# A cross-attention kernel with a second, token-driven attention: token weighing, gathers and low parts moved among heads and engines

## The reference

```python
query = hidden_states @ Wq                       # (2, 1024, 640), 8 heads of 80
keyt, valt = enc @ Wk, enc @ Wv                  # enc: 2044 rows of the context
hs = _mha(query, keyt, valt)                     # the large attention
ca_q1 = jnp.einsum('btc,th->bch', ca, Wq_ca)     # ca: the last 4 rows of the context
indices = np.linspace(0, 383, 1024).astype(np.int64)
ca_q1 = ca_q1[:, indices, :]                     # 384 distinct rows, repeated to 1024
ca_hs1 = _mha(ca_q1, residual, residual)         # residual = hidden_states
ca_q2 = ca_hs1 @ Wq
ca_hs2 = _mha(ca_q2, ca @ Wk_ca, ca @ Wv_ca)     # only 4 keys
out = (hs + ca_hs2) @ Wout + b_out + residual
```

## Time and profile before

| | |
|---|---|
| median of 3 runs | 1190.87 us (1190.83 to 1190.9) |
| profiled execution | 1190.76 us |
| its span, first to last instruction | 1188.9 us |
| TensorE busy | 1181.1 us, 99% |
| VectorE busy | 855.1 us, 72% |
| ScalarE busy | 680.5 us, 57% |
| GpSimd busy | 111.9 us, 9% |

### The profile page before, as it was taken

One profiled execution on the slowest core, in us unless ns is written; L12 is line 12 of the kernel. 1 busy time (PEld: TensorE's weight loads), 2 busy tenths in 40 slices (PEclk: granted clock), 3 DMA queues, 4 the chain that ended last, 5 costly groups with the idle time before them and its releaser, 6 DMA issues.

```text
span 1188.9 us, 14961 instructions
## 1 busy us (share of the span) xinstructions
PE 1181.1 (99%) x5633; PEld 968.2 (81%) x5633; DVE 855.1 (72%) x1226; ACT 680.5 (57%) x797; POOL 111.9 (9%) x125
## 2 busy tenths in 40 slices
PE   9999999999999999999999999999999999999999
PEld 8888888788666678888888888888888888887998
DVE  7468625771144399989989989989899898986541
ACT  5323433222644477777777777777777777778210
POOL 1100000011000010100100110110110000000332
PEclk9999999999999999999999999999999999999999
DMA  8975785592930075264354455445436437432363
GB/s 312 354 273 178 257 312 200 219 345 96 295 67 1 1 170 130 67 157 111 86 138 111 102 122 122 104 109 138 108 90 157 94 83 167 124 68 67 107 215 133
DMA packets 140146, 178.08 MB, mean 150 GB/s; under 512 B 80729, under 2 KB 97881, under 8 KB 136234
## 3 DMA queue, kind: packets, MB, share of 16 engines
q1 hardware_dynamic: 132458, 156.34, 46.5%
q10 hardware_dynamic: 4752, 10.55, 2.7%
q0 software_dynamic: 2864, 10.24, 2.6%
HBM read 113.66 MB, written 63.28 MB: 149 GB/s over the span
## 4 chain that ended last, share of the span: by engine, by line
PE 94%; DVE 2%; DMA 1%; issue 1%; ACT 1%; SPq 1%; DVEq 0%; ACTq 0%
PE at_ps L1343 28%; PE bank L732 20%; PE at_ps L1314 19%; PE at_ps L255 9%; PE acc_t_ps L1095 7%; PE at_ps L1537 6%; PE s_ps L1063 2%; PE bank L709 1%; DVE prob_lo L1189 1%; DMA x_f<-in_xT 1%; PE acc_t_ps L1074 1%; PE f_ps L255 1%; PE f_ps L1016 1%; PE f_ps L1026 0%; PE at_ps L1540 0%
## 5 line engine op out<-in xcount | busy, mean ns | idle before, releaser
L264 DVE TENSOR_REDUCE mpart<-at_ps 128x1 f32<-128x512 f32 x480 | 326.4, 685 | 51.9 <-PE at_ps L255 51.4
L1254 ACT ACTIVATE prob_hi<-at_ps 128x1024 fp32r<-128x1024 f32 (+1 forms) x256 | 263.7, 1030 | 171.3 <-PE at_ps L1314 170.7
L1189 DVE TENSOR_TENSOR prob_lo<-probs,prob_hi 128x1024 fp32r<-128x1024 f32 (+1 forms) x256 | 311.8, 1218 | 20.4 <-ACT probs L1259 20.2
L1343 PE MATMUL at_ps<-prob_hi,v 128*128 128x512 f32 x1024 | 310.1, 389 | 0.0
L1259 ACT ACTIVATE probs<-at_ps 128x1024 f32<-128x1024 f32 (+1 forms) x256 | 261.4, 1021 | 0.0
L1343 PEld LDWEIGHTS at_ps<-prob_hi,v 128*128 128x128 f32 x1024 | 192.1, 188 | 40.2 <-issue 0.3
L255 PE MATMUL at_ps<-a 128*128 128x512 f32 x480 | 187.5, 391 | 0.5 <-DVE mpart L264 0.5
L1314 PE MATMUL at_ps<-a 128*128 128x512 f32 x512 | 158.3, 390 | 0.8 <-DMA b<-mrow 0.4
L1343 PE MATMUL at_ps<-prob_lo,v 128*128 128x512 f32 x512 | 157.8, 389 | 0.1
L1314 PE MATMUL at_ps<-b 128*128 128x512 f32 x512 | 157.7, 389 | 0.0
L1314 PEld LDWEIGHTS at_ps<-a 128*128 128x128 f32 x512 | 95.8, 188 | 21.8 <-DMA b<-mrow 1.4
(11 more groups left out here) (153 smaller groups left out, 1336.1 us busy)
## 6 DMA issues: line engine op xcount, KB each, us to landing
v_hi_d<-v_t SPq DMA_DIRECT2D x16, 648.0 KB, 6.4
v_lo_d<-v_t SPq DMA_DIRECT2D x16, 648.0 KB, 8.0
v<-v_hi_d SPq DMA_DIRECT2D x16, 648.0 KB, 5.9
v<-v_lo_d SPq DMA_DIRECT2D x16, 648.0 KB, 7.7
k_hi_d<-out_hi SPq DMA_DIRECT2D x40, 256.0 KB, 5.0
k_lo_d<-out_lo SPq DMA_DIRECT2D x40, 256.0 KB, 6.2
a<-k_hi_d SPq DMA_DIRECT2D x16, 640.0 KB, 7.7
b<-k_hi_d SPq DMA_DIRECT2D x16, 640.0 KB, 11.4
```

The costliest lines, as they stand in the source:

```text
L264: dve.tensor_reduce(self.mpart[:, g % 2, qt, c:c + 1], at[:, 0:w], AX, ALU.max).then_inc(self.mx_done, 1)
L1189: eng.tensor_tensor(pl[n % PL][0:r, :], prob[n % PF][0:r, :], ph[n % PB][0:r, :].bitcast(F32), ALU.subtract).then_inc(sem, 1)
L1254: act.activation(ph[n % PB][0:r, :], s_ps[n % 2][0:r, :], ACT.Exp, scale=SCALE).then_inc(ph_done, 1)
L1343: mm = pe.matmul(wide[3][:, u], a[:, t, :], y[:, u * CH:(u + 1) * CH], start=t == 0 and m == 0, stop=t == KT - 1 and m == 2)
```

## The change

The second weighing, both gathers and their copies leave the seam. `gather(pe, i, to)` and `gather_out(dve, i, to)` now run in the last head, behind tiles 1 and 3 (`GATHER_AT`), through the PSUM banks of the maxima; the copy to `p2g` is VectorE's, not ScalarE's. The second `exp2` stands between ScalarE's exp(0) and exp(1), and `weigh` for batch 0 on VectorE at the end of tile 3 of head 0 (`WEIGH_AT`). GpSimd makes the lows of tiles 4, 6, 8 and 10 of head 0 (`POOL_T`). `early_split` takes its ten steps in tiles 2 to 11 of the last head (`SPLIT_FROM`) instead of 6 to 15. GpSimd and SP no longer wait for the gathers at the seam but for `vw` and the one-hot matrix; the output stage waits for the gathers. `p2g` lies in the place of `ca_f`, and `onehot`, `p2` and the fold's tensors have places of their own. The work itself stays the same.

```diff
+SPLIT_FROM = 2
-POOL_T = ()
+POOL_T = (4, 6, 8, 10)
+WEIGH_AT = 3
+GATHER_AT = (1, 3)
...
@@ tokens
-            raw_out(len(heads) - 1)
-            vw_out(0)
-            first_copy()
-            exp2(1)
-            vw_out(1)
+            for u in range(2):
+                vw_out(u)
+
+        def last_exp(act):
+            exp2(act, 1)
...
             center(order[1])
-            weigh(1, order[1])
             low_vw(1)
...
-            pe.wait_ge(oh_done, 1)
             pe.wait_ge(at.mx_done, STEPS)
             fold_values(0)
             token_scores(len(heads) - 1)
-            first_gather()
             fold_values(1)
...
+        def gather(pe, i, to):
+
+            b = order[i]
+            pe.wait_ge(oh_done, 1)
+            pe.wait_ge(p2_zero, 2)
+            pe.wait_ge(p2_done, i + 1)
+            pe.wait_ge(at.mx_done, G * STEPS)
+            if i:
+                pe.wait_ge(g_done, i)
             for c, a, z in spans:
-                mm = pe.matmul(s_ps[b][:, a // CH, a % CH:a % CH + z - a],
+                mm = pe.matmul(to[:, a // CH, a % CH:a % CH + z - a],
                                p2[:, b, c].rearrange("p r h t -> p (r h t)"),
                                onehot[:, a:z], start=True, stop=True)
             mm.then_inc(g_full, 1)
 
+        def gather_out(dve, i, to):
+            dve.wait_ge(g_full, i + 1)
+            dve.tensor_copy(kept["p2g"][:, order[i], :], to[:].rearrange("p u n -> p (u n)")).then_inc(g_done, 1)
+
+        def last_weigh(dve):
+            weigh(dve, 1)
+
+        def last_fold(pe):
+
+            pe.wait_ge(step, folded(len(heads) - 1))
...
@@ attend
-        on_pool = [n % KT in POOL_T and n < N - KT for n in range(N)]
+        on_pool = [n in POOL_T for n in range(N)]
...
             exp(0)
-            last_copy(act)
+            tokens_end.last_exp(act)
             exp(1)
...
-                if g == G - 1 and t < KT - 3:
+                if n == WEIGH_AT:
+                    tokens_end.last_weigh(dve)
+                if g == G - 1 and t in GATHER_AT:
+                    dve.wait_ge(wout_lo, MC)
+                    tokens_end.gather_out(dve, GATHER_AT.index(t), wide[1])
+                if g == G - 1:
                     early_split(dve, t)
-            for t in range(KT - 3, KT):
-                early_split(dve, t)
...
             second_loaded(0)
-            gathered(pe, 1)
             scores(0, lambda: None)
-            last_gather(pe)
-            folded_values(pe)
+            tokens_end.folded_values(pe)
             scores(1, lambda: None)
+            tokens_end.last_fold(pe)
...
                 if n == 0:
                     values(n, lambda: None)
-                    gathered(pe, B)
...
                 if n:
                     values(n, between)
+                if n >= N - KT and n % KT in GATHER_AT:
+                    tokens_end.gather(pe, GATHER_AT.index(n % KT), wide[1])
...
@@ output
-            first = KT - 2 * MC
+            first = SPLIT_FROM
...
-            if t >= first:
+            if first <= t < first + 2 * MC:
...
                 if n == 0:
-                    pe.wait_ge(at.mx_done, G * STEPS)
+                    tokens_end.gathered(pe, B)
```

More of the change, by code:

```diff
@@ L74, in products @@
     return ((a[0], b[0]), (a[0], b[1]), (a[1], b[0]))
+@dataclass
+class TokensEnd:
+    folded_values: Callable
+    one_hot: Callable
+    last_exp: Callable
+    last_weigh: Callable
+    last_fold: Callable
+    gather: Callable
+    gather_out: Callable
+    gathered: Callable
 @dataclass
@@ L784, in tokens @@
         raw = kept["raw"]
[L785 to L788, removed]
+        rden, s2, t2, r2 = kept["fold"]
         f_ps = [s.psum(f"f_ps{i}", [P, CH]) for i in range(2)]
@@ L909, in scalar, with chained, weigh @@
                 if n == NH:
-                    exp2(0)
+                    exp2(act, 0)
             raw_out(len(heads) - 1)
-            vw_out(0)
-            first_copy()
-            exp2(1)
-            vw_out(1)
[L917 to L921, removed]
-        def vector(dve):
[L924 to L930, removed]
+            for u in range(2):
+                vw_out(u)
+        def last_exp(act):
+            exp2(act, 1)
+        steps = [0]
+        def chained(dve, ins):
+            steps[0] += 1
+            ins.then_inc(step, 1)
+            dve.wait_ge(step, steps[0])
+        def weigh(dve, i):
+            b = order[i]
+            v = s2[:, b].rearrange("p c (h t) -> p (c h) t", t=NT)
+            dve.wait_ge(e2_done, i + 1)
+            chained(dve, dve.tensor_reduce(t2[:, b, :], v, AX, ALU.add))
+            chained(dve, dve.reciprocal(r2[:, b, :], t2[:, b, :]))
+            by = r2[:, b, :].rearrange("p (c h) -> p c h", c=KC)[:, :, :, None].to_broadcast([P, KC, NH, NT])
+            w = s2[:, b].rearrange("p c (h t) -> p c h t", t=NT)
+            chained(dve, dve.tensor_tensor(w, w, by, ALU.mult))
+            for r in range(2):
+                chained(dve, dve.tensor_copy(p2[:, b, :, b + r], w))
+            dve.tensor_tensor(p2[:, b, :, b + 2], w, p2[:, b, :, b].bitcast(F32), ALU.subtract).then_inc(p2_done, 1)
+        def vector(dve):
             def fold(n):
@@ L946, in center @@
                 v = s2[:, b].rearrange("p c (h t) -> p (c h) t", t=NT)
-                chained(dve.tensor_reduce(t2[:, b, :], v, AX, ALU.max))
+                chained(dve, dve.tensor_reduce(t2[:, b, :], v, AX, ALU.max))
                 dve.tensor_tensor(v, v, t2[:, b, :, None].to_broadcast([P, KC * NH, NT]),
                                   ALU.subtract).then_inc(d2_done, 1)
[L951 to L961, removed]
             def low_vw(u):
@@ L1001, in vector @@
                     if n == NH + 1:
-                        weigh(0, order[0])
+                        weigh(dve, 0)
             low_vw(0)
@@ L1377, in attend, with output @@
         return Stage(sync, gpsimd, scalar, vector, tensor)
-def output(nc, outer, kept, at, wout, d, scratch, out):
+def output(nc, outer, kept, at, wout, tokens_end, d, scratch, out):
     with ExitStack() as stack:
@@ L1619, in program @@
         attending = attend(nc, s, kept, at, wout, tokens_end, d, scratch)
-        ending, prefetch, early_split = output(nc, s, kept, at, wout, d, scratch, out.rearrange("b s n -> (b s) n"))
+        ending, prefetch, early_split = output(nc, s, kept, at, wout, tokens_end, d, scratch, out.rearrange("b s n -> (b s) n"))
         with nc.Block() as block:
```

47 lines of the change are left out of this document (20 added, 27 removed).

## The result

The change makes the kernel slower: 1208.6 us median (1208.45 to 1208.78, four runs) against 1190.86 (1190.83 to 1190.9, four runs). The ratio is 1.0143, with an interval of 1.0131 to 1.0155. The direction was forecast, the size was not: 17.7 us instead of 4.20, and outside the range. The profiled execution took 1208.78 us, its span 1207.0.

The account below looks back on a forecast made before the run. TensorE, busy for 99% of the span, was taken as the bound, so time is its matmuls plus gaps. Terms -1.08 + 1.19 - 0.20 + 1.24 + 1.04 - 0.34 + 2.35 = +4.20 on 1190.87 gave 1195.0 us, range 1191.5 to 1196.6.

Parts of the forecast that it names:

- the unit: All TensorE stages: a matmul of 512 columns starts 0.227 us after the one before, taken as unchanged by the change.
- The seam: Between the tokens' stage and the heads: earlier fold and vw copies let scores(2) start at 419.82, not 420.90: -1.08 us.
- The weighing in tile 3: First head: VectorE's 1.79 us second weighing delays maxima, so pieces 12 and 13 wait in TensorE: +1.19 us.
- GpSimd's lows: First head: four lows of 2.3 to 2.5 us leave VectorE, removing small lateness of later pieces: -0.20 us (0 to -0.3).
- The gathers' matmuls: Last head, behind tiles 1 and 3: TensorE pays 0.62 us twice, +1.24.
- VectorE's lateness in the last head: Gather copies and slowed splits use up VectorE's spare; TensorE waits at lows 251, 252 and 253: +1.04 us with restarts.
- The old stall at the last low: End of the last head: no split behind tile 11, so TensorE's wait and restart at 1108.74 go: -0.34 us.
- The collision: End of the last head: GpSimd's two bias additions alternate with lows 253 to 255 on the SBUF port: +2.35 us.
- Rival 1: End of the last head: VectorE keeps the port, GpSimd's additions come behind low(255): +1.85, 1192.7 us; chance 0.20.
- Rival 2: First and last heads: VectorE has room, maxima and lateness don't hold TensorE; not slower: -0.46, 1190.4 us; chance 0.14.
- rival 3: More port clashes: GpSimd's lows hold the weighing or maxima, or both additions run in one piece: +5.0 to +6.5, 1196.5; chance 0.12.

Follow-up runs that it names:

- the aligned form: The changed kernel with a pad of 352 bytes ahead of a0, so that a0, a1 and b0 start at multiples of 512 bytes again: 1194.99 us, ratio 1.0029.
- the kernel before with the 160 bytes alone: The kernel before with 160 unused bytes ahead of a0, so that a0, a1 and b0 start 160 bytes past a multiple of 512: 1204.64 us, ratio 1.0115.

## Why the prediction was wrong, point by point

- **The step that failed** is the unit: "A matmul of 512 columns starts 0.227 us after the one before it; that is my unit", together with "The new places in SBUF ... change no order that the timelines show as tight". The new places were looked at for the order of loads and stores alone. They changed the unit itself: the heads took 708.13 us and in the aligned form 694.91 (419.88 to 1114.79), 13.2 more, or 4.3 ns for each of 3040 matmuls. The prediction had this term at nothing. Of the 14.0 between the two spans nearly 0.7 more was lost in the output stage, whose inputs are split into `a0`, `a1`, `b0` and others; the kernel before with the 160 bytes alone loses as much there (78.9 us for 78.2). "A change that moves work between the other engines can only close or open gaps" was the root of it: this change also moved tensors.
- The seam: -1.02 measured, -1.08 forecast. The wait for the last fold and the earlier vw copies came as described.
- The weighing in tile 3: +1.06 for +1.19. The missing 0.13 is as much as the weighing itself was shorter (1.66 for 1.79).
- GpSimd's lows: they took 2.38 to 2.40 (2.38 to 2.42 in the change as it is), inside 2.3 to 2.5, and the maxima beneath them ran at full speed. But the lateness that they were to take away stays: small waits of 0.26 us after tile 6 became 0.22. -0.20 was too much, the bound at 0 was right.
- The gathers' matmuls: 0.53 twice, +1.07 for +1.24 (1080.44 to 1080.97 and 1085.53 to 1086.06 in the aligned kernel). The copies out of PSUM took 1.23 and 1.22 for 1024 elements, the single rate of the earlier trace rows. The prediction read the table of the Trainium skill (VectorE: DVE Perf Modes, The perf-mode tier table) as allowing double rate; the same section goes on to say that with fp32 an operand in PSUM holds the copy to single rate, and this trace agrees.
- VectorE's lateness in the last head: in the aligned kernel TensorE waits at lows 251, 252 and 253, 0.16, 0.22 and 0.22 with a restart of 0.11 each, 0.93 together for +1.04. In the change as it is, where TensorE is slower, low 251 waits no more. The old stall at the last low is gone, -0.36 for -0.34.
- The collision: +2.26 for +2.35, by the starts; 2.45 by taking it away. Rival 1, for which VectorE would keep the port, falls: each addition got in ahead of the next low.
- The sum of these is 3.9, the aligned kernel's span says 4.1. So the mechanisms were right, and that its median of 1194.99 meets 1195.0 to the hundredth is luck: single terms were off by up to 0.17, in both directions. The direction of the whole change was right for these 4 us; most of the 17.7 came from a cost that the prediction had not seen. Rival 2 falls with pieces 12 and 13, rival 3 with the maxima under GpSimd's lows.

What the forecast lacked was a rival in which TensorE's own instructions change their price. Nothing in the trace of before could give that price; but a list of the places before and after would have shown three operands leaving the multiple of 512 on which all nine stood, and that was worth a rival, or at least a wider range on the side of slower.

## What to carry to other kernels

When an edit moves or adds buffers, compare the start addresses of all operands of the hot matmuls before and after, modulo 256 bytes, and keep them alike: here, with TensorE busy for 99% of the time, 4 ns a matmul (13.2 us) outweighed all the waits that the edit moved (4.1 us). When a kernel is slower by more than its waits explain, read the mean time of untouched lines first. And before work is given to GpSimd, ask which short operation of VectorE's on a critical chain would be issued beneath it: `mneg`, 0.17 us long by itself, stood for what was left of GpSimd's low.

## What the runs showed of the hardware

- Matmuls of 512 columns in float32 forms ran 0.227 us apart when the starts of all operands agreed modulo 256 bytes, at whatever remainder (0 and 64 were tried), and about 0.230 to 0.232 apart when some tensors differed by 32, 64, 128 or 160; by the ratios the loss was 0.67 to 1.22% of the whole, for 3040 matmuls. Loaded weights counted like streamed operands, and matmuls whose own operands agreed were slowed as well; in one head two such matmuls of twelve, reading from elsewhere, slowed the loop to 0.2317.
- A one-input scalar operation of VectorE on 128x8 numbers stood until a GpSimd subtraction of 128x1024 ended, 1.63 us for 0.17; a reduction in SBUF to 128x8 numbers under the same subtraction took its 0.19.
- GpSimd's subtraction of 128x1024 took 2.38 to 2.42 us.
- VectorE with three subtractions of 128x1024 queued and GpSimd with two additions of 128x640, all of two inputs in SBUF, took turns, one whole instruction each: 6.23 us for 3.68, and 4.81 for 3.11.
